# A selective-scan layer: the drives of nine instead of eight of sixteen units come from the tensor engine

## The reference, cut to what matters

```python
dt = softplus(dt_lo @ W_dt.T + dt_b)
A = -exp(A_log)
def step(h, inp):
    xt, dtt, Bt, Ct = inp
    dA = exp(dtt[:, :, None] * A)                      # the decay
    h = dA * h + (dtt * xt)[:, :, None] * Bt[:, None, :]   # the drive is added
    y = einsum('ben,bn->be', h, Ct)
    return (h, y)
...
x1 = mamba(xn, m1...); x2 = flip(mamba(flip(xn), m2...))
x = x + ga * (layernorm(x1 + x2) + xn)
h = layernorm(x) * (1 + cb) + sb
h = silu(lin(h, w1)) * lin(h, w2); h = gelu(lin(h, h1)); h = gelu(lin(h, h2))
x = x + gb * lin(h, w3)
```

## Time and profile before

| | |
|---|---|
| median of three runs | 12,999.88 us |
| the profiled execution, its own time | 13,003.51 us |
| its span (first to last instruction) | 13,001.7 us |
| VectorE busy | 12,010.2 us (92%) |
| GpSimd busy | 11,539.1 us (89%) |
| ScalarE busy | 10,850.5 us (83%) |
| tensor engine busy (matmuls) | 10,179.6 us (78%) |
| mean granted clock of the tensor engine | 0.885 |
| mean busy share of the DMA engines by queue 1 | 33.9% |

### The profile page before, as it was taken

One profiled execution on the slowest core, in us unless ns is written; L12 is line 12 of the kernel. 1 busy time (PEld: TensorE's weight loads), 2 busy tenths in 40 slices (PEclk: granted clock), 3 DMA queues, 4 the chain that ended last, 5 costly groups with the idle time before them and its releaser, 6 DMA issues.

```text
span 13001.7 us, 179153 instructions
## 1 busy us (share of the span) xinstructions
PE 10179.6 (78%) x51228; PEld 5796.2 (45%) x51228; DVE 12010.2 (92%) x7080; ACT 10850.5 (83%) x23452; POOL 11539.1 (89%) x5988
## 2 busy tenths in 40 slices
PE   5667877788787887878878787887878878778777
PEld 2334544444444444544445444444444445444445
DVE  5999999999999999999999999999999999999992
ACT  5788888888888898888888888888888988888883
POOL 4899999999999999999999999899999999999992
PEclk7788988889898898988989888898989989889898
DMA  2223333333333333333333333333333333333332
GB/s 83 83 84 109 118 108 123 119 105 115 109 126 109 114 121 102 125 110 118 118 109 116 107 124 118 107 115 108 124 110 115 120 104 127 108 118 117 110 109 96
DMA packets 605385, 1450.11 MB, mean 112 GB/s; under 512 B 68400, under 2 KB 109504, under 8 KB 599792
## 3 DMA queue, kind: packets, MB, share of 16 engines
q1 hardware_dynamic: 604272, 1437.26, 33.9%
HBM read 1346.70 MB, written 90.31 MB: 111 GB/s over the span
## 4 chain that ended last, share of the span: by engine, by line
PE 28%; ACT 23%; issue 21%; DVE 16%; POOL 11%; DMA 1%; DVEq 0%; SPq 0%; POOLq 0%; ACTq 0%
DVE state L1242 10%; PE driven L867 9%; POOL state L1272 8%; ACT state L1054 8%; ACT v_sb L1067 8%; PE y_ps L881 5%; PE q_ps L822 4%; DVE driven L1231 3%; PE q_ps L809 2%; PE p_ps L730 2%; PE b_ps L857 2%; ACT L1054 1%; POOL v_sb L1347 1%; PE p_ps L738 1%; PE p_ps L754 1%
## 5 line engine op out<-in xcount | busy, mean ns | idle before, releaser
L1272 POOL TENSOR_TENSOR state<-state,c_rep 128x1024 f32<-128x1024 f32 x4096 | 9671.1, 2385 | 1050.9 <-DVE state L1242 1048.4
L1242 DVE TENSOR_TENSOR_SCAN state<-state,driven 128x1024 f32<-128x1024 f32 x4096 | 9107.5, 2271 | 512.9 <-PE driven L867 313.4
L1054 ACT ACTIVATE state<-ud_rep,cols_sb 128x512 f32<-128x512 f32 x8192 | 5180.4, 709 | 2.2
L1067 ACT ACTIVATE v_sb<-u_t,b_t 128x128 f32<-128x128 f32 x12288 | 3980.1, 505 | 1190.3 <-PE driven L867 1186.0
L867 PE MATMUL driven<-consts_sb,v_sb 128*128 128x128 f32 x16384 | 2638.2, 314 | 1636.0 <-DVE state L1242 1602.1
L867 PEld LDWEIGHTS driven<-consts_sb,v_sb 128*128 128x128 f32 x16384 | 2133.9, 161 | 3279.2 <-DVE state L1242 2196.2
L881 PE MATMUL y_ps<-state,consts_sb 128*32 128x512 f32 x16384 | 2492.0, 684 | 511.2 <-POOL state L1272 508.4
L1231 DVE TENSOR_TENSOR driven<-ud_rep,b_ps 128x1024 f32<-128x1024 f32 x2048 | 2390.2, 1213 | 16.3 <-DMA ud_rep<-ud_rows 16.3
L822 PE MATMUL q_ps<-hid,wq_sb 128*128 128x256 f32 x7936 | 2061.9, 405 | 191.4 <-ACT hid L1032 124.1
L822 PEld LDWEIGHTS q_ps<-hid,wq_sb 128*128 128x128 f32 x7936 | 1481.5, 196 | 906.7 <-issue 709.3
L1347 POOL TENSOR_TENSOR v_sb<-u_t,b_t 128x512 f32<-128x512 f32 x1024 | 1159.6, 1132 | 13.2 <-ACT u_t L980 13.2
(11 more groups left out here) (139 smaller groups left out, 5543.2 us busy)
## 6 DMA issues: line engine op xcount, KB each, us to landing
c_rep<-bc_rows SPq DMA_DIRECT2D x2048, 256.0 KB, 3.0
ud_rep<-ud_rows SPq DMA_DIRECT2D x512, 512.0 KB, 4.0
wq_sb<-in_h SPq DMA_DIRECT2D x512, 512.0 KB, 3.8
wq_sb<-in_f SPq DMA_DIRECT2D x128, 512.0 KB, 4.1
wp_sb<-in_win SPq DMA_DIRECT2D x64, 512.0 KB, 4.5
dt_sb<-conv_taps SPq DMA_DIRECT2D x32, 1024.0 KB, 5.7
ud_rows<-u_pad SPq DMA_DIRECT2D x128, 256.0 KB, 3.5
ud_rows<-dt_sb SPq DMA_DIRECT2D x128, 256.0 KB, 3.4
```

The source lines that it names most:

```text
L1054: ins = act.activation(state[:, unit % STATE_RING, j, :], ud_rep[:, nth % 2, j, 1, :], ACT.Exp, scale=a_neg[:, d, c, j, g:g + 1])
L1067: ins = act.activation(v_sb[:, unit // 2 % V_RING, tt, :, :, n].rearrange("p j e -> p (j e)"), u_t[:, nth % 2, tt, :], ACT.Identity, scale ...
L1242: dve.tensor_tensor_scan(flat, flat, driven[:, q % DRIVE_RING].rearrange("p j t -> p (j t)"), 0.0, ALU.mult, ALU.add).then_inc(scanned, 1)
L1272: pool.tensor_tensor(part, part, c_rep[:, unit % ROW_RING, :].unsqueeze(1).to_broadcast([P, 2, T]), ALU.mult).then_inc(was_read, 1)
```

## The change

The units that the tensor engine drives are no longer the odd ones. They are given by their place in a cycle of 16: 1, 3, 5, 7, 8, 10, 12, 14, 15. VectorE drives the other seven. The counts on semaphores follow (`pe_units`, `dve_units`). ScalarE's copies move: at each unit u it makes block 2 of unit u + 2, block 1 of u + 3 and block 0 of u + 4, where these are the tensor engine's, and it makes them between the decays of the two halves of unit u + 2.

```diff
-DRIVE_RING, STATE_RING, ROW_RING, V_RING, V_AHEAD, POOL_AHEAD = 2, 4, 2, 2, 5, 3
-PE_UNITS = tuple(range(1, UNITS, 2))
-DVE_UNITS = tuple(range(0, UNITS, 2))
+DRIVE_RING, STATE_RING, ROW_RING, V_RING, V_AHEAD, POOL_AHEAD = 2, 4, 2, 2, 4, 3
+CYCLE, PE_OF_CYCLE = 16, (1, 3, 5, 7, 8, 10, 12, 14, 15)
...
+def by_pe(unit):
+    return unit % CYCLE in PE_OF_CYCLE
+
+def pe_units(unit):
+    return unit // CYCLE * len(PE_OF_CYCLE) + sum(k < unit % CYCLE for k in PE_OF_CYCLE)
+
+def dve_units(unit):
+    return unit - pe_units(unit)
...
         def v_free(at, unit):
-            return of_body(at, 2 * len(PE_UNITS), 2 * (unit // 2 - V_RING + 1)) + 2 * V_RING
+            return of_body(at, 2 * pe_units(UNITS), 2 * (pe_units(unit) - V_RING + 1)) + 2 * V_RING
...
                 for unit in range(UNITS):
-                    to_drive, ends_pass = scans and unit + 1 in PE_UNITS, unit % NG == 0
+                    to_drive, ends_pass = scans and unit + 1 < UNITS and by_pe(unit + 1), unit % NG == 0
...
                     if to_drive:
                         drive(at, unit + 1, 1)
-                        if unit + 2 < UNITS:
-                            spread(at, unit + 2)
-                        elif at.has("next"):
-                            spread(at, unit + 2)
+                    if not by_pe(unit + 2) and (scans if unit + 2 < UNITS else scans and at.has("next")):
+                        spread(at, unit + 2)
                     side(at, unit)
...
-            def make_v(at, unit, part):
+            def make_v(at, unit, tt):
...
-                for tt in (2, 1) if part else (0,):
-                    for n in range(NN):
-                        ins = act.activation(v_sb[:, unit // 2 % V_RING, tt, :, :, n].rearrange("p j e -> p (j e)"),
+                for n in range(NN):
+                    ins = act.activation(v_sb[:, pe_units(unit) % V_RING, tt, :, :, n].rearrange("p j e -> p (j e)"),
...
                 for unit in range(UNITS):
-                    if unit % 2 == 0:
-                        if in_scan(at, unit + 2):
-                            decays(at, unit + 2, 0)
-                            decays(at, unit + 2, 1)
-                        if in_scan(at, unit + V_AHEAD):
-                            make_v(at, unit + V_AHEAD, 0)
-                    else:
-                        if in_scan(at, unit + V_AHEAD - 1):
-                            make_v(at, unit + V_AHEAD - 1, 1)
-                        if in_scan(at, unit + 2):
-                            decays(at, unit + 2, 0)
-                            decays(at, unit + 2, 1)
+                    if in_scan(at, unit + 2):
+                        decays(at, unit + 2, 0)
+                    for tt in (2, 1, 0):
+                        ahead = unit + V_AHEAD - tt
+                        if by_pe(ahead) and in_scan(at, ahead):
+                            make_v(at, ahead, tt)
+                    if in_scan(at, unit + 2):
+                        decays(at, unit + 2, 1)
                     side(at, unit)
...
-                        if unit + 1 < UNITS and unit + 1 in DVE_UNITS or unit + 1 == UNITS and at.has("next"):
+                        if not by_pe(unit + 1) and (unit + 1 < UNITS or at.has("next")):
                             drive(at, unit + 1, 0)
                             drive(at, unit + 1, 1)
...
-                    if unit % 2 == 0 and (at.kind in SCAN_PARTS if ahead < UNITS else at.has("next")):
+                    if by_pe(ahead) and (at.kind in SCAN_PARTS if ahead < UNITS else at.has("next")):
                         make_v(at, ahead)
```

34 lines of the change are left out of this document (18 added, 16 removed).

## The result

| | before | after |
|---|---|---|
| median of 4 runs each, us | 13,002.23 (12,999.0 to 13,006.67) | 13,153.08 (13,147.23 to 13,154.52) |
| profiled span, us | 13,001.7 | 13,145.4 |
| mean granted TensorE clock | 0.885 | 0.882 |

The changed kernel takes 151 us more: ratio 1.0114, interval 1.0098 to 1.013. The forecast was 12,915, in a range from 12,790 to 13,120.

The account below looks back on a forecast made before the run. VectorE was taken to set the pace wherever it does not wait. Per batch -17.9 + 4.5 + 5 + 4 - 3 + 2 = -5.4 us, -86 over 16 batches, gave 12,915 us, in a range from 12,790 to 13,120.

Parts of the forecast that it names:

- VectorE's saving: VectorE: two drives fewer per 16 units save 2.24 us, 17.9 per batch; 4.5 given back where other engines are full.
- Capping the gain by the idle time of the other engines: Stretches of the batch: shortening limited to idle time minus added work on GpSimd and ScalarE; 4.5 us per batch given back.
- ScalarE's new order: ScalarE: copies between the decay halves shorten VectorE's 9.8 us wait for decays by a third, -3 us per batch.
- ScalarE's twelve copies: ScalarE: twelve more copies per 16 units, 3.74 us, or 29.9 per batch; counted within the 4.5 given back.
- The pairs: Neighbouring tensor-engine units: drives late behind side steps, 5 us per batch, plus 4 for the half clock, 2 for GpSimd's lag.
- units 45, 70, 93 and 102: Pairs behind these units have one and a half or two side steps between; most of the `driven` wait expected there.
- half-clock term: Tensor engine: a fifth of 16 pairs at 1.2 GHz run late; 0 to 15 us per batch, taken as 4.
- C: Rival: tensor-engine side steps wait for ScalarE and pace the pairs; slower, 13,065 to 13,170 us; chance 0.26.
- A: Rival: nearly the full VectorE gain, pairs fit and ScalarE's order removes waits; 12,650 to 12,735, up to 12,840; chance 0.14.
- B: Rival: no change, within 1.6 us of zero per batch; the next engine takes what one is spared; chance 0.20.
- D: Rival: VectorE and GpSimd keep each other out, each added `v_sb` block stops VectorE 1.04 us; 13,048 us; chance 0.03.
- units 16 to 31: Sign: this stretch with idle engines must shorten by at least 1 us, or the forecast is wrong.

Follow-up runs that it names:

- experiment 9: Kernel before, with VectorE's two drives of the unit at place 8 cut to 8 of each 512 columns: 12,949.03 us, ratio 0.9961.
- Experiment 1: Changed kernel's ScalarE order, but with the eight odd units driven by the tensor engine as in the kernel before: 13,078.19 us, ratio 1.0061.
- experiment 5: Changed kernel's nine units, each product begun when its buffer is free (4 or 5 units ahead), behind both halves of the decays: 13,067.13 us, ratio 1.0055.
- 6: As experiment 5, with 11 of ScalarE's 12 copies for the unit at place 8 left out: 13,032.8 us, ratio 1.0029.
- Experiment 10: Eight units of 16 with one tensor-engine pair (7 and 8) and one VectorE pair per cycle, ScalarE's order as in experiment 5: 13,110.19 us, ratio 1.0087.
- Experiment 7: As experiment 5, with the tensor engine's side steps at places 6 and 13 cut to their last matmul or transpose: 12,996.84 us, ratio 0.9998.
- experiment 14: Kernel before, with experiment 9's VectorE cut and the tensor engine's side steps at places 6 and 13 cut: 12,922.03 us, ratio 0.9946.
- 13 to 18: Kernel before, with work cut at GpSimd alone or at two to four of VectorE, ScalarE, tensor engine and GpSimd: 12,845.52 to 12,937.0 us.
- experiments 2 and 3: Changed kernel with products one unit earlier; both decay halves ahead of the copies in 2 (13,960.27 us), kept apart in 3 (14,719.28 us).
- 15: As experiment 14, with 11 of ScalarE's 12 copies for place 7 also left out: 12,932.36 us, ratio 0.9951.
- 18: As 15, with GpSimd's two multiplications of place 8 also halved, so all four engines are cut: 12,845.52 us, ratio 0.9883.
- 16: Kernel before, with GpSimd's two multiplications of the unit at place 8 cut to 256 of each 512 columns: 12,913.5 us, ratio 0.9935.

## Why the prediction was wrong

Two steps failed: that VectorE's spared time shows, and that ScalarE's new order helps.

**VectorE's saving, -17.9 + 4.5 per batch: wrong, and by this account the largest error.** The step that failed is "Nothing else is that full for that long, so VectorE sets the pace wherever it does not wait". The instructions were counted and priced rightly (1792 drives, busy 11,692 against about 11,710 forecast). But experiment 9 finds that 0.23 of spared VectorE time shows; if that share, measured on the kernel before, holds for the 318 us of this change, it is 73 us, 4.6 per batch instead of 13.4. Capping the gain by the idle time of the other engines, stretch by stretch, was no substitute: it asks how much of an engine's time is free, not whether the free time lies where it is needed.

**ScalarE's new order, -3 per batch: wrong in sign.** Its reasoning on decays held: VectorE's wait for them fell from 10.7 to 2.1 us per batch, more than the third that I took off. What the step left out is the product itself. It was complete 13 to 15 us ahead before and -1.1 to 3.6 us ahead after, and the drive that waits for it has the tensor engine's sums and side steps queued behind. Experiment 1 measures the order at +79, that is +4.9 per batch, where the forecast has -48 us. This lies at the end of the bounds (+5), for another reason than the one given there. It is the most directly measured of the terms: the same order, without pairs and without a copy more.

**ScalarE's twelve copies.** The forecast counted them within the 4.5 given back. Experiments 5 and 6 give 34 us, 2.1 per batch.

**The pairs, 5 + 4 + 2 per batch: not shown wrong, and not measured apart.** After has 16 pairs of the tensor engine's in a batch. What is left for them is a remainder: experiment 5 is 72 us above before, of which the copies are 34, and VectorE's saving takes off 73 by the share above; so 111 us remain, 6.9 per batch or 0.43 a pair, below the 11 forecast. Experiment 10 also measured 111, but with half as many such pairs, together with eight of VectorE's; were all of it the price of the tensor engine's pairs, 16 would cost 13.9 per batch, above the 11. That the two numbers agree is chance. Experiment 7 shows that side steps at these places are part of it: 70 us less without them, against 23 for the same cut with single units (14 against 9). The places were wrong: units 45, 70, 93 and 102 were to hold most of the wait for `driven`; in after the largest are before units 120, 88 and 108, with 6.3, 5.5 and 4.8 us per batch, and 108 is in no pair. At unit 88 it was not two whole side steps that made it late, but one that stood for ScalarE and then ran at the half clock, and the product beside it. The reason for taking the half-clock term low, that in a pair the tensor engine doesn't idle, fails at that unit; its frequency was taken too high all the same: of the drives at place 8 about one in six began at the low clock, of those at place 15 none, where the forecast had a fifth of all pairs.

The sum per batch is then -4.6 + 4.9 + 2.1 + 6.9 = +9.3 us, 149 in all, against 151 measured. It is no check: the last term is what the others leave over, and with experiment 10's price for each pair the sum would be 261. Shown are the two parts, 79 for the order and 72 for nine units; how the 72 divide is worked out, not shown.

**The rivals.** C had the side, the size (13,065 to 13,170) and its sign in the profile, a wait for `driven` above 600 us (735) spread over all cycles. Unit 88 shows its mechanism, a side step that waits for ScalarE with the drive right behind. But as a whole C was right in good part by luck: experiment 1 reaches 578 us of this wait and half of the loss with no pair at all, and a pair costs 0.43 us by the remainder and 0.87 at most, where C decides only from 0.84, a point worked out with VectorE's full saving. A falls with experiment 9. B's reason, that the next engine takes what one is spared, is nearest to what experiment 9 shows, though 13 to 18 find no single such engine; I gave it 0.20. D falls: GpSimd's blocks took 1.07 us each on average, and scans and drives kept their length.

Of the signs named, VectorE's counts and busy time were right. ScalarE was busy 11,252 instead of 11,340. The wait for decays fell further than to the 110 forecast (31 us), but the wait for `driven` did not stop at 500, and units 16 to 31 lengthened, which was the sign that the forecast is wrong.

## What to carry to other kernels

Neither the busy share nor the chain's share priced a microsecond here: VectorE (92% busy, 16% of the chain) was worth 0.23, GpSimd (89%, 11%) 0.32, ScalarE (83%, 23%) 0.06. Before a gain is booked where several engines are nearly full, cut the work alone and measure. Ask of each producer that is moved how long before its use it finishes (a timeline shows it), which queue stands for it when that lead is gone, and whether its buffer is free if it is to start earlier. Removing a wait is no gain in itself: ScalarE's 1186 us for a free buffer were the sign of a healthy lead, and the kernels that brought it to 525 and to 29 were slower. More of it is no gain either: at 2046 and 2913 us, in experiments 2 and 3, the decays stood behind it. And when a price comes from an experiment, count how often it holds the thing priced: 10 had half as many pairs as the change.

## What the runs showed of the hardware

With fewer side steps on the tensor engine the granted clock of the profiled execution was lower: 0.871 in experiment 14, 0.865 in 15 and 0.879 in 18, against 0.885 of the kernel before. It also moved where the tensor engine's own work was untouched: 0.880 with VectorE's cut alone (9), 0.891 with GpSimd's (16). Part of a saving can thus come back as slower matmuls: those of the sum (`y_ps`) took 707 ns on average in 14, before 684. How much of the kernel's time that is wasn't measured.

A load of ScalarE's table costs 1.28 us, with the next instruction starting within 0.02 us of its end, at both loads at unit 88; around one activation of the network that is 2.56 us in which no copy or decay can go ahead.

GpSimd's reads kept their length beside VectorE's scans in every run (2.37 to 2.40 us on average), and its blocks took 1.05 to 1.14. The VectorE instruction of the earlier trace rows, with two inputs in SBUF, did not: its mean went from 2.69 us (16) to 5.24 (14) with no change to it, while the scans stayed at 2.27. That GpSimd's work beside it is the reason, as the earlier trace rows suggests, wasn't tested.
